# Two more pairs of rounds per chunk whose narrow exponentials go partly to GpSimd, and GpSimd's root ahead of its block

## The reference

```
h = layernorm(x) * (1 + ca) + sa
q = per head (16 heads of 16 features): h_head @ Wq_head.T
attn = softmax(q q.T / NORM)              # 4096 x 4096 for each head, queries = keys = values = q
x = x + ga * ((attn @ q) @ Wp.T + bp)
h = layernorm(x) * (1 + cb) + sb
z = silu((layernorm(h) * gamma + beta) @ w1 + b1) @ w2 + b2
x = x + gb * (h + 0.5 * z)
```

## Time and profile before

| | |
|---|---|
| time, median of 3 runs | 1959.11 us (1958.48 to 1961.0) |
| the profiled execution | 1958.2 us, span 1956.4 us |
| ACT busy | 1880.3 us, 96% |
| PE busy | 1868.9 us, 96% |
| DVE busy | 1490.3 us, 76% |
| POOL busy | 1251.7 us, 64% |
| L890, wide exponentials | 683 of 1886 ns |
| L896, narrow exponentials | 682, 665.9 us |

### The profile page before, as it was taken

How to read it: one execution, slowest core, us unless ns; L and a number is a source line. 1 busy time by engine, 2 the same in 40 slices (tenths; PEclk the granted TensorE clock), 3 DMA queues, 4 the chain that set the end, 5 groups by cost and what they waited for, 6 DMA issues and landing times.

```text
span 1956.4 us, 47545 instructions
## 1 busy us (share of the span) xinstructions
PE 1868.9 (96%) x18411; PEld 544.5 (28%) x18411; DVE 1490.3 (76%) x2543; ACT 1880.3 (96%) x1491; POOL 1251.7 (64%) x2118
## 2 busy tenths in 40 slices
PE   8788889999999999999999999999999999999999
PEld 6211112222222222222232222322232222322225
DVE  5567677778878877777887788778777778777884
ACT  6899999999999999999999999999999999999992
POOL 5173777477746776377873778467763768737770
PEclk9899999999999999999999999999999999999999
DMA  6531212122121221212112121112121121111100
GB/s 214 163 93 45 51 34 54 43 59 49 51 49 40 57 52 51 57 44 53 50 47 56 54 49 54 37 55 54 47 56 46 52 48 54 49 38 43 43 7 18
DMA packets 121391, 108.40 MB, mean 55 GB/s; under 512 B 21952, under 2 KB 120128, under 8 KB 120912
## 3 DMA queue, kind: packets, MB, share of 16 engines
q1 hardware_dynamic: 120416, 103.69, 19.8%
q10 hardware_dynamic: 752, 1.67, 0.2%
HBM read 96.49 MB, written 8.65 MB: 54 GB/s over the span
## 4 chain that ended last, share of the span: by engine, by line
ACT 50%; PE 28%; issue 12%; DVE 4%; POOL 2%; DVEq 0%; POOLq 0%
ACT attend_probs L890 29%; ACT attend_probs L896 20%; PE attend_sums L943 14%; PE attend_scores L929 8%; PE attend_out L951 3%; PE attend_scores L951 1%; ACT hidden L884 1%; PE attend_sums L957 1%; PE attend_out L957 1%; DVE attend_probs L1148 1%; DVE attend_spare L1160 1%; POOL attend_spare L858 1%; DVE attend_probs L1149 0%; DVE base L1184 0%; DVE attend_sums_sb L1114 0%
## 5 line engine op out<-in xcount | busy, mean ns | idle before, releaser
L890 ACT ACTIVATE attend_probs<-attend_scores 128x2048 f32<-128x2048 f32 x683 | 1288.3, 1886 | 8.6 <-PE attend_scores L929 8.4
L943 PE MATMUL attend_sums<-attend_probs,values 128*17 128x512 f32 x8192 | 1007.0, 597 | 2.1 <-POOL attend_probs L863 1.6
L1148 DVE COPY attend_probs<-attend_scores 128x896 f32<-128x896 f32 x578 | 630.0, 1090 | 282.8 <-PE attend_scores L929 276.1
L896 ACT ACTIVATE attend_probs<-attend_probs 128x896 f32<-128x896 f32 (+1 forms) x682 | 665.9, 976 | 5.3 <-DVE attend_probs L1148 3.1
L929 PE MATMUL attend_scores<-asks,keys 64*128 64x512 f16 x4096 | 564.5, 381 | 72.8 <-ACT attend_probs L890 66.8
L854 POOL TENSOR_TENSOR attend_spare<-attend_spare 128x256 f32<-128x256 f32 x289 | 183.0, 633 | 373.9 <-DVE attend_spare L1162 373.8
L929 PEld LDWEIGHTS attend_scores<-asks,keys 64*128 64x128 f16 x4096 | 151.2, 94 | 671.2 <-ACT attend_probs L890 543.3
L943 PEld LDWEIGHTS attend_sums<-attend_probs,values 128*17 128x17 f32 x8192 | 174.8, 96 | 507.4 <-issue 483.3
L858 POOL TENSOR_TENSOR attend_spare<-attend_spare 128x256 f32<-128x256 f32 x289 | 232.6, 805 | 24.1
L863 POOL TENSOR_TENSOR attend_probs<-attend_spare 128x256 f32<-128x256 f32 x289 | 219.4, 759 | 22.7
L861 POOL TENSOR_TENSOR attend_spare<-attend_spare,attend_probs 128x256 f32<-128x256 f32 x289 | 212.3, 735 | 24.1
(11 more groups left out here) (163 smaller groups left out, 838.7 us busy)
## 6 DMA issues: line engine op xcount, KB each, us to landing
keys<-parts_dram SPq DMA_DIRECT2D x768, 64.0 KB
keys<-parts_dram SPq DMA_DIRECT2D x256, 56.0 KB
asks<-parts_dram SPq DMA_DIRECT2D x192, 64.0 KB
start_x_in<-L_attn_x SPq DMA_DIRECT2D x8, 512.0 KB, 9.5
parts_dram<-start_q_parts SPq DMA_DIRECT2D x16, 256.0 KB, 2.6
attend_x_now<-L_attn_x SPq DMA_DIRECT2D x8, 512.0 KB, 4.1
out<-base SPq DMA_DIRECT2D x15, 256.0 KB, 2.6
asks<-parts_dram SPq DMA_DIRECT2D x64, 56.0 KB
```

What stands on the lines that cost most here:

```text
L890: act.activation(place(n, 2), ps_scores[:, 0:4, :], ACT.Exp, scale=scale).then_inc(exps_done, 1)
L896: act.activation(cols, cols, ACT.Exp, scale=scale).then_inc(exps_done, 1)
L943: last = pe.matmul(ps_sums[32 * hq:32 * hq + E1, :], values[:, j + STEPS * b, (gg % Q_GROUPS) * Q_HEADS + hq, :], place(gg * PAIRS + Q_HEA ...
L1148: dve.tensor_copy(flat(n, 0, DIRECT), bank[:, 0:DIRECT]).then_inc(copied, 1)
```

## The change

The narrow `norm` stretch begins at r = 16 instead of 12, so two more pairs of rounds per chunk (chunks 1 to 7) have spare columns: 14 pairs, 303 in place of 289. By the pairing that is (12,13) and (14,15) in chunks 1, 3, 4, 6 and 7, and (11,12) and (13,14) in chunks 2 and 5. On GpSimd the root of a round now stands ahead of the block of the same round. On VectorE, at r = 13 of these groups, `spare_parts` stands behind `norms`.

```
@@ is_busy
-    norm = c > 0 and group == 0 and 12 <= r <= 20
+    norm = c > 0 and group == 0 and 16 <= r <= 20
@@ GpSimd's loop
                 for at in range(ROUNDS):
+                    if at in MOMENTS_IN:
+                        power(*MOMENTS_IN[at], slice(0, GT))
                     for k, (first, last) in enumerate(SPARE_PAIRS):
                         if last == at + BEHIND:
                             exps(k, first)
-                    if at in MOMENTS_IN:
-                        power(*MOMENTS_IN[at], slice(0, GT))
@@ VectorE's loop
-                        spare_parts(at + BEHIND)
+                        if c == 0 or group != 0 or r != 13:
+                            spare_parts(at + BEHIND)
                         if at in PIECE_IN:
                             after_piece(*PIECE_IN[at])
                         if c > 0 and group == 0:
                             norms(c - 1, r)
+                        if c > 0 and group == 0 and r == 13:
+                            spare_parts(at + BEHIND)
```

## The result

The changed kernel took 1962.21 us (median of 22 runs), the kernel before, run beside it, 1959.39 us (22 runs): a ratio of 1.0014 with a 95% interval of 1.0008 to 1.0020. It is slower, by 2.8 us, which is under the 0.2% (3.9 us) that the forecast of "slower" asked for, and less than half of the 6.1 us forecast. Executions that ran far longer than the others of their kernel are left out of the medians and ratios in this text: two of the run with the root behind the block (2346.43 us, at a granted clock of 0.76, and 4660.38 us) and one of the kernel before (2150.23 us, at 0.849).

A forecast was written before the change was run, and what follows sets the result against it. ScalarE was taken to set the pace, with VectorE's copy in a narrow window. Savings included, 3 x 1.00 + 2 x 0.75 + 2 x 0.78 = 6.1 us on 1959.1 gave 1965.2 us, range 1956 to 1970.

The forecast's parts named there:

- slower: Whole kernel: more than 0.2% (3.9 us) over the time before, chance 0.63.
- What bounds, and the window: Rounds 12 to 16: ScalarE sets the pace; VectorE's copy must start 1.01 to 1.47 us after the last L896.
- Chunks 1, 4, 7: Pairs (12,13) and (14,15): L896 of round 16 at 347.04, before 346.04, so +1.00 us a chunk.
- round 15's chain of turns: Round 15, chunk 1: VectorE and GpSimd instructions alternate from L1160 to the second L1204, so copy 16 starts at 345.78.
- Chunks 3, 6: Same pairs, residual a round earlier: L896 of round 16 at 804.43, before 803.68, so +0.75 us a chunk.
- Chunks 2, 5: Round 14: root's L848 and block's L854 hold centring; L896 of round 15 at 572.78, before 572.00, +0.78 us a chunk.
- Moving the root ahead of the block ... costs nothing by itself.: GpSimd's new order: no cost of its own; in chunks 1, 3, 4, 6, 7 L848 stays ready before round 16's L1213.
- Who holds whom: VectorE and GpSimd wait each other out, then take their own time less some 0.14 us; L1204 held like L1162.
- 12 of 12 turns: Trace before, L1260 then L1160: all 12 places where L863 came while L1260 ran gave GpSimd the next turn.
- Not slower: Rival: L1204 takes no turn with GpSimd, -1.1 us, 1958.0 us; chance 0.18.
- TensorE waits instead: Rival: VectorE keeps its turns, GpSimd's block slides, TensorE waits up to 1.9 us in round 16; 1960.7 us, chance 0.07.
- Chances: Whole kernel: slower 0.63, same 0.33, faster 0.04; the forecast's own course 0.70.

The follow-up runs named there:

- the run with the root behind the block: Changed kernel with only GpSimd's order put back, a pair's block ahead of the same round's root: 1959.00 us against 1958.74 before, ratio 1.0000.
- the first block short: Changed kernel, GpSimd's block for pair (12,13) in chunks 1, 3, 4, 6, 7 cut to four instructions on 4 columns (work left out): 1955.41 us, one run.
- the root behind the second block: Changed kernel, but in chunks 2 and 5 GpSimd takes round 13's root behind the block of (13,14): 1965.26 us, one run.

## Why the prediction was wrong in size, and where it was right

- **What bounds, and the window.** Right. The L896 of chunk 1 were forecast for 334.97, 337.80, 340.40, 343.00 and 347.04 on the clock of before; with the 2.44 us by which this execution ran late (337.41 against 334.97) they came at 334.97, 337.78, 340.39, 343.00 and 346.75. The stall in round 16 has its place and its reason; its size in chunk 1 was forecast at 1.44 us over the due 345.60 and is 1.15.
- **Chunks 1, 4, 7.** +1.00 us forecast, +0.71 measured. The term that was too large is round 15's chain of turns: L1160 was to wait for L859 to its end, but L859 ended at 345.21, and L1160 started at 345.24 and ran its free 0.29 us. This is the turn that the prediction named as the kind that can go either way, and it is half of the 0.29 us. The other half: from L863's end to that of the second L1204, 1.16 us were reckoned (344.70 to 345.86) and 1.04 measured (346.99 to 348.03).
- **Chunks 3, 6.** +0.75 us forecast, +0.84 measured.
- **Chunks 2, 5: the step that failed.** "L1162 569.56, L848 570.44, L1204 570.78": the prediction let the root's 1.02 us hold the centring as a block's instruction does, +0.78 us a chunk. It holds nothing that shows; the chunks gained their whole 0.41 us. Two times 1.19 us are 2.4 of the 3.1 us between the forecast's 6.1 and the groups' 3.0. The prediction read no row for this meeting, took the price from rows of other instructions, and gave it no bound from the other side. The trace of before had such a row, in the layer norm behind the last round (L1403 has the form of L1204; the root is on 2 columns there, and the last two rows show it with no two-input instruction beside it):

```profile
1918.34 0.88 DVE L1403 SCALAR_TENSOR_TENSOR attend_hid<-attend_x,attend_mo,mod 128x256 f32<-128x256 f32 x2
1918.39 0.48 POOL L846 TENSOR_SCALAR attend_v_eps<-attend_mo 128x2 f32<-128x2 f32 x1 [14.91 <-DVE attend_mo L1387]
1918.95 0.83 POOL L848 TENSOR_TENSOR attend_rs<-attend_v_eps,attend_minus_half 128x2 f32<-128x2 f32 x1
...
1921.93 0.19 POOL L846 TENSOR_SCALAR attend_v_eps<-attend_mo 128x2 f32<-128x2 f32 x1 [2.14 <-DVE attend_mo L1387]
1922.20 0.70 POOL L848 TENSOR_TENSOR attend_rs<-attend_v_eps,attend_minus_half 128x2 f32<-128x2 f32 x1
```

  L846 and L848 are lengthened there and the two L1403 keep 0.88 us. So half of the step was right, that the root waits for VectorE, and the half that VectorE then waits for the root was wrong.
- **"Moving the root ahead of the block ... costs nothing by itself."** Wrong. The run with the root behind the block shows it to cost 3.2 us, more than the whole change: of GpSimd's work in these rounds the root is the one piece that centring can run beside unheld, and moved ahead it pushes the block into that place. The sum had the effect in it, but not as the price of this part.
- **Who holds whom.** Right for L1204 beside a block, which no row of before showed: 472 to 942 ns over the 28, where it was never over 481. From the list by line of the changed kernel (count, ns min/median/max):

```profile
L1204 DVE SCALAR_TENSOR_TENSOR attend_hid<-attend_x,attend_mo,mod x28: 472/611/942, 342.5 to 1729.8; 128x256 f32<-128x256 f32 x28
```

  That a waiting GpSimd instruction gets its turn between two neighbours of VectorE held in round 15, with the first block short, and with the root behind the second block. (The prediction's 12 of 12 turns are 11 of 11 in the trace: of the 22 places, L863 was held by L1260 in 11, held L1260 in seven, and made no difference in the other four.) The page of the Trainium skill, SBUF — State Buffer, section Who interferes with whom, is borne out for the seven instructions of a block: in the changed kernel each of them held an L1162, an L1204 or an L1213, which ended 0.27 to 0.29 us behind it. (L1160 reads one tensor, so of the prediction's two rows only L1162's bears on that rule.) For L848 the rule holds in one direction, L848 waits; in the other it does not: L848 reads SBUF too, and by the page's rule would have held L1204 for the rest of its 1.12 us; the trace has L1204 at 0.48 us beside it, and the measurement decides.
- **Rivals.** "Not slower" did not come: L1204 was held. "TensorE waits instead" came as a hidden second wait (0.71 us in chunk 1) and became the first one where the vector wait was taken away, 0.39 us in two chunks.
- **Chances.** The measured +2.8 us is clear of no change by its interval, but lies inside the 0.2% (3.9 us) that the prediction counted as the same, at 0.33; 0.63 of slower by over 0.2% was too sure, since one term that rested on no row of its own, the root's hold, swung the sum by 2.4 us of 6.1.

Still open: why the root does not hold. Its size counts, and not the operation alone: a TENSOR_SCALAR of GpSimd on 256 columns (L855) held an L1204 that was issued while it ran to 0.61 to 0.62 us in five places of the changed kernel, while one on 4 columns (L846) left L1162 at its free 0.42 to 0.43 us. Whether it goes by the columns or by the time in which an instruction moves data, and where between 4 and 256 columns the hold sets in, no run here shows; nor did L848's operation, a power, run on many columns.

## What to carry to other kernels

Where one engine copies for a pacing engine inside a window of some tenths of a microsecond, price added work on a helper engine by the turns it takes from the copier, not by its own length: here the same vector instructions (L1160, L1162 and two L1204 of round 15) took 0.29 + 0.83 + 1.70 = 2.8 us with the helper's block running, and 0.29 + 0.43 + 1.23 = 1.95 us without it, the last with one turn left. Look for the helper's piece of work that holds nobody and put that beside the crowded stretch. And a term that rests on no row belongs in the forecast with both its ends, above all when the sum swings by two fifths on it.

## What the runs showed of the hardware

- An instruction of GpSimd on 256 columns and a VectorE instruction with two SBUF inputs excluded each other, and waiting ones alternated: in round 15 L1162 took 0.83 us (0.43 free) and two L1204 took 1.70 (0.87 free).
- One of GpSimd on 2 or 4 columns waited for such a VectorE instruction (L858 0.46 us where 0.19 is free, L846 0.48 where 0.19, L848 1.12 where 1.02), but did not hold it: L1204 stayed at 0.48 us beside it.
- The copies out of PSUM were not held: the 176 L1148 of the changed kernel that were issued while an L854 ran took 1.07 to 1.09 us.
